# Second expert routing moved into attention, with expert rows and results scattered by indirect DMA

## The reference

```python
x = x + 0.5 * ffn(layernorm(x))      # mixture of experts
x = x + attention(layernorm(x))      # convolution, 8 heads, blocks of 128 tokens
x = x + 0.5 * ffn(layernorm(x))      # the same experts again

def ffn(x):                          # 8 experts, hidden width 176
    h = x.reshape(-1, 256)
    probs = softmax(h @ router_w.T)
    vals, idx = top_k(probs, 2)
    vals = vals / vals.sum(axis=-1, keepdims=True)
    ...
    for each expert e:
        gate, up = split(h @ gup[e].T)
        out += combine[:, e] * ((silu(gate) * up) @ dp[e].T)
```

## Time and profile before

| | us |
|---|---|
| three runs | 907.18, 909.76, 909.19 (median 909.19) |
| the profiled execution, as timed | 907.88 |
| its span in the profile | 905.7 |
| mean granted TensorE clock | 0.905 of 2.4 GHz |

### The profile page before, as it was taken

The page is one execution under the profiler, slowest core; times in us unless marked ns, Lnnn a source line. Parts: engine busy times, 40 slices in busy tenths (PEclk is TensorE's granted clock), DMA queues, the critical chain, the costliest instruction groups (busy, mean ns, idle before and its releaser), DMA issues. The chain is left out here.

```text
span 905.7 us, 20908 instructions
## 1 busy us (share of the span) xinstructions
PE 677.2 (75%) x5582; PEld 613.6 (68%) x5614; DVE 571.1 (63%) x1593; ACT 438.6 (48%) x1624; POOL 398.6 (44%) x449
## 2 busy tenths in 40 slices
PE   3760679999995899999999999852599999950000
PEld 3760569999994678788888888752599999950000
DVE  6668946666665667667676676649666666633333
ACT  1350036666663567677676767640056666630000
POOL 2054645445425544434434321203554444427765
PEclk9999999999996999999999999965599999985555
DMA  9910024444432111111111100000034444424444
GB/s 327 249 60 0 0 79 132 127 130 131 132 100 75 54 42 42 38 48 41 43 38 41 46 20 13 19 24 0 23 115 127 131 127 130 127 84 140 130 135 128
DMA packets 56143, 78.12 MB, mean 86 GB/s; under 512 B 9235, under 2 KB 45973, under 8 KB 56085
## 3 DMA queue, kind: packets, MB, share of 16 engines
q1 hardware_dynamic: 43028, 41.65, 14.1%
q0 software_dynamic: 13056, 35.67, 14.1%
HBM read 45.83 MB, written 31.46 MB: 85 GB/s over the span
## 5 line engine op out<-in xcount | busy, mean ns | idle before, releaser
L495 POOL DMA_INDIRECT shared<-h_rows,stage x144 | 137.7, 956 | 129.2 <-issue 76.0
L528 POOL TENSOR_TENSOR pr<-pr,prec 128x1024 f32<-128x1024 f32 x32 | 60.7, 1897 | 156.0 <-DVE prec L949 156.0
L749 DVE SCALAR_TENSOR_TENSOR x_sb<-yg,wts,x_sb 128x256 f32 (+1 forms) x128 | 62.1, 485 | 71.9 <-DMA yg<-y_rows,cstage 50.1
L1087 PE MATMUL CC<-w_hi,rowsT_hi 128*128 x288 | 106.5, 370 | 0.0
L1087 PE MATMUL CC<-w_lo,rowsT_hi 128*128 x288 | 93.9, 326 | 0.0
L1087 PE MATMUL CC<-w_hi,rowsT_lo 128*128 x288 | 93.8, 326 | 0.0
L648 ACT ACTIVATE pr<-SS,nmax 128x128 f32<-128x128 f32 x256 | 90.6, 405 | 0.1
L861 DVE TENSOR_TENSOR shared<-shared,CC 128x176 f32<-128x176 f32 x144 | 48.6, 337 | 59.4 <-ACT shared L573 43.0
L573 ACT ACTIVATE shared<-CC 128x176 f32<-128x176 f32 x144 | 45.8, 318 | 74.5 <-PE CC L1087 71.5
L540 POOL DMA_INDIRECT yg<-y_rows,cstage x64 | 62.7, 980 | 35.7 <-POOL cstage L535 25.2
L515 POOL DMA_INDIRECT yg<-y_rows,cstage x64 | 62.9, 983 | 23.8 <-issue 16.8
(11 more groups left out here) (211 smaller groups left out, 1983.3 us busy)
## 6 DMA issues: line engine op xcount, KB each, us to landing
y_rows<-shared SPq DMA_DIRECT2D x144, 128.0 KB
x_sb<-in_x_dram SPq DMA_DIRECT2D x4, 1024.0 KB, 8.7
h_rows<-hr SPq DMA_DIRECT2D x32, 128.0 KB, 1.7
out_dram<-x_sb SPq DMA_DIRECT2D x16, 256.0 KB
w_lo<-in_gupT_dram SPq DMA_DIRECT2D x1, 2816.0 KB
shared<-h_rows,stage POOLq DMA_INDIRECT x144
h_rows<-h_ring SPq DMA_DIRECT2D x2, 1024.0 KB, 5.4
h_rows<-pr SPq DMA_DIRECT2D x2, 1024.0 KB, 6.4
```

Of the source, the lines that this page charges most:

```text
L495: pool.indirect_dma_start(out=rows[:, u, :], out_offset=None, in_=h_dram[:, :], in_offset=bass.IndirectOffsetOnAxis(ap=stage[:, k, u:u + 1 ...
L528: pool.tensor_tensor(pr[:, q, :, :], pr[:, q, :, :], prec[:, q, :].unsqueeze(2).to_broadcast([P, NH, P]), ALU.mult).then_inc(t["norm"], 1)
L749: st.did(v.scalar_tensor_tensor(out=x_tile(t), in0=yg[:, q, k, :], scalar=wts[:, k, bass.ds(t, 1)], in1=x_tile(t), op0=ALU.mult, op1=ALU.add))
L1087: i = pe.matmul(CC[:, 512 * (u % 2):512 * (u % 2) + GU], rows_part[:, u % 2, c * P:(c + 1) * P], weights, start=(n == 1), stop=(n == 3 * DC))
```

## The change

**Routing inside attention.** The second routing stage is gone. In the turns that `PICKS` lists, VectorE selects the two experts for four blocks at once (`pick`; for two or one at the end), TensorE counts by small matmuls how many earlier tokens chose the same expert, VectorE fetches these ranks (`read_ranks`) and works out a row number (`place`). Each expert has a region of `REGION` rows in a new DRAM tensor `h_regions`, so no slot has to be known: the row is the expert's region plus the rank. In the turns that `SENDS` lists GpSimd scatters each block's rows there, once for each of its two experts. A row carries two more numbers, so it is 258 wide: twice its token's number, and its first expert. `hr` is a ring of eight in place of two and is no longer stored by SP. After attention `finish_route` works out where each slot tile begins, and SP writes eight tiles of padding behind the experts' rows; eight more are written at the start of attention.

**Expert stage.** SP loads each tile of rows contiguously from its region, at an address from a register. A new operation on VectorE (`y_to`) works out from the two extra numbers to which row each result goes, twice the token's number plus 0 or 1. GpSimd scatters the results there (`send_sums`). Padding rows get a number out of bounds and are left out.

**Last sum.** The results lie in token order, so SP loads them contiguously, two blocks at a time, into the place of the expert weights, which are no longer needed. No ring limits these loads.

**Loops.** Attention is written out turn by turn, and six expert steps stand ahead of the loop in place of two.

The core of the diff:

```diff
...
+        PICKS = {9: (0, 4), 13: (4, 4), 17: (8, 4), 21: (12, 4), 25: (16, 4), 29: (20, 4), 31: (24, 2), 33: (26, 2),
+                 35: (28, 2), 36: (30, 1), 37: (31, 1)}
+        SENDS = {**{b + 10: (b,) for b in range(16)}, 26: (16, 17), 27: (18, 19), 30: (20, 21), 31: (22, 23, 24, 25),
+                 33: (26, 27), 35: (28, 29), 36: (30,), 37: (31,)}
...
+        def turns(turn):
+            for i in range(FIRST_TURN, LAST_TURN):
+                turn(i)
...
+                regs = [sp.alloc_register(f"pad_at{e}") for e in range(E)]
+                sp.load(regs, pad_i[0:1, :])
+                for e in range(E):
+                    at = sp.snap(regs[e], min_val=e * REGION, max_val=e * REGION + TOKENS)
+                    sp.dma_start(h_regions[bass.ds(at, P), :], pad_rows[:, :]).then_inc(T["pads"], 16)
+
...
+                        if s >= RING:
+                            sp.wait_ge(r["rowsT"], s + 1)
+                            sp.wait_ge(r["dest"], s - RING + 1)
+                        sp.dma_start(rows[:, s % RING, :], h_regions[bass.ds(at, P), :]
+                                     ).then_inc(r[f"g{s % RING}"], 16)
+
+            def load_sums():
+                for g in range(TILES // 2):
+                    sp.dma_start(y_pairs(g), y_tokens[:, 2 * g:2 * g + 2, :]).then_inc(y_in[g // 2], 16)
...
             end_phase(sp, 2)
-            store_second()
+            fill_spare()
+            fill_pads()
             end_phase(sp, 3)
+            load_rows(1)
             end_phase(sp, 4)
-            store_y(1)
-            end_phase(sp, 5)
+            load_sums()
...
+                with pool.Fori(0, SLOT_TILES // RING) as j:
+                    for u in range(RING):
+                        pool.wait_ge(r["y_sb"], RING * j + u + 1 + 2)
+                        pool.sem_inc(r["gate_pool"], 1)
+                        pool.wait_ge(r["dest"], RING * j + u + 1)
+                        pool.sem_inc(r["gate_pool"], 1)
+                        pool.indirect_dma_start(
+                            out=y_dram[0:TOPK * TOKENS, :],
+                            out_offset=bass.IndirectOffsetOnAxis(ap=y_dest[:, u:u + 1], axis=0),
+                            in_=y_sb[:, u, :], in_offset=None, bounds_check=TOPK * TOKENS - 1, oob_is_err=False
+                        ).then_inc(r[f"st{u}"], 16)
+                for u in range(RING):
+                    pool.wait_ge(r[f"st{u}"], 16 * (SLOT_TILES // RING))
...
+                    for b in SENDS.get(i, ()):
+                        q = b % GROUP
+                        pool.wait_ge(t["dest"], b + 1)
+                        pool.sem_inc(t["gate"], 1)
+                        for k in range(TOPK):
+                            pool.indirect_dma_start(
+                                out=h_regions[:, :],
+                                out_offset=bass.IndirectOffsetOnAxis(ap=dest[:, q, k:k + 1], axis=0),
+                                in_=hr[:, q, :], in_offset=None).then_inc(t[f"sent{q}"], 16)
...
+                for t in range(TILES):
+                    if t % 4 == 0:
+                        v.wait_ge(y_in[t // 4], 32)
+                    for k in range(TOPK):
+                        st.did(v.scalar_tensor_tensor(out=x_tile(t), in0=y_pairs(t // 2)[:, t % 2, k * D:(k + 1) * D],
+                                                      scalar=wts[:, k, t:t + 1], in1=x_tile(t),
+                                                      op0=ALU.mult, op1=ALU.add))
+                        st.wait()
+                    v.sem_inc(final, 1)
...
+            def finish_route(L):
+                r, t = R[L], T
...
+                step(v.tensor_tensor(passed, etcum[:, :].unsqueeze(1).to_broadcast([P, SLOT_TILES, E]),
+                                     iota_f[:, 0:SLOT_TILES].unsqueeze(2).to_broadcast([P, SLOT_TILES, E]), ALU.is_le))
+                step(v.tensor_reduce(expert_of[:, :], passed[:, :, 0:E - 1], AX.X, ALU.add))
...
+                step(v.scalar_tensor_tensor(out=row_i[:, :], in0=iota_f[0:1, 0:SLOT_TILES], scalar=float(P),
+                                            in1=eidf[:, :], op0=ALU.mult, op1=ALU.add))
...
+                def y_to(u, s, grp):
+                    q = u % RING
+                    v.wait_ge(r[f"g{q}"], 16 * (grp + 1))
+                    after(v, r[f"st{q}"], 16 * grp)
+                    v.scalar_tensor_tensor(out=y_dest[:, q:q + 1], in0=rows[:, q, D + 1:D + 2],
+                                           scalar=expert_of[:, bass.ds(s, 1)], in1=rows[:, q, D:D + 1],
+                                           op0=ALU.not_equal, op1=ALU.add).then_inc(r["dest"], 1)
...
                 def step(u, s, j):
                     if is_tile(s + 1):
                         rows_low((u + 1) % 2, s + 1)
+                        if send:
+                            y_to(u + 1, s + 1, (u + 1) // RING + j)
                     if is_tile(s):
                         hid_s(u % 2, s)
                     if is_tile(s - 1):
...
+                def pick(first, n):
...
+                    v.wait_ge(t["lg"], first + n)
+                    v.sem_inc(passed_dve, 1)
+                    for j in range(at_4, at_4 + n):
+                        ins = v.max(best4[:, j, :], lg4[:, j, :])
+                    step(ins)
+                    step(v.tensor_tensor(oh4[:, of, :, :],
...
+                    v.tensor_tensor(sel4[:, of, :], oh4[:, of, 0, :], oh4[:, of, 1, :], ALU.add
+                                    ).then_inc(t["picked"], n)
+                    v.tensor_scalar(region4[:, of, :], pick4[:, of, :], float(REGION), float(E * REGION),
+                                    ALU.mult, ALU.add)
+
...
+                def read_ranks(first, n):
+                    of = slice(first % 4, first % 4 + n)
+                    v.wait_ge(t["ranked"], first + n)
+                    v.tensor_tensor(rank4[:, of, :, :], oh4[:, of, :, :],
+                                    G[:, D:D + n * E].rearrange("p (i e) -> p i e", e=E).unsqueeze(2)
+                                    .to_broadcast([P, n, TOPK, E]), ALU.mult).then_inc(t["ranks_read"], n)
...
+                def place(first, n):
+                    at_4, q = first % 4, first % GROUP
+                    of = slice(at_4, at_4 + n)
+                    v.wait_ge(t["ranks_read"], first + n)
+                    st.did(v.tensor_reduce(place4[:, of, :], rank4[:, of, :, :], AX.X, ALU.add))
...
+                    v.tensor_tensor(dest[:, q:q + n, :], region4[:, of, :], place4[:, of, :], ALU.add
+                                    ).then_inc(t["dest"], n)
...
                                         negate=True).then_inc(t["max"], 1)
+                    if i in PICKS:
+                        pick(*PICKS[i])
+                    if placed(i, False):
+                        place(*placed(i, False))
...
+                    if i in PICKS:
+                        read_ranks(*PICKS[i])
+                    if placed(i, True):
+                        place(*placed(i, True))
...
+                    if i in PICKS:
+                        first, n = PICKS[i]
+                        at_4 = first % 4
+                        pe.wait_ge(t["picked"], first + n)
+                        after(pe, t["res"], upto(i - 1))
+                        if i > 35:
+                            pe.wait_ge(t["dest"], first)
+                        pe.matmul(G[:, D:D + n * E], before_bf[:, :], sel4[:, at_4:at_4 + n, :], start=True, stop=False,
+                                  skip_group_check=True)
+                        for j in range(n - 1):
...
+                        pe.matmul(G[:, D:D + n * E], ones_bf[:, :],
+                                  so_far[:, :].unsqueeze(1).to_broadcast([P, n, E]), start=False, stop=True,
+                                  skip_group_check=True).then_inc(t["ranked"], n)
+
+                turns(turn)
+                pe.wait_ge(t["dest"], TILES)
+                pe.matmul(G[:, D:D + E], ones_bf[:, :], so_far[:, :], start=True, stop=True).then_inc(t["counted"], 1)
...
```

272 lines of the change are left out of this document (165 added, 107 removed).

## The result

The changed kernel takes 967.9 us (median of four runs, 963.9 to 971.5) against 909.0 us for the kernel before beside it. The ratio is 1.065, with a 95% interval of 1.060 to 1.070. The forecast was 929 us and the range 888 to 960: the sign was right, the size was not, and the time lies outside the range. The profiled execution has a span of 967.6 us, timed at 969.3.

The account below looks back on a forecast made before the run. VectorE was taken to bound the second routing, TensorE the second expert stage. The sum 905.7 - 3 + 70 - 46 = 926.7, with 2.2 around the span, gave 929 us; range 888 to 960.

Parts of the forecast that it names:

- Part 1: Up to the second expert stage's first transposes: gain 3 us; a gain of 18 or loss of 12 not excluded.
- rival (c): Routing in attention not hidden: scatters delay every turn's normalisation, or the tail is longer; 15 us more, 944 us; chance 0.12.
- Part 2: Second expert stage: tiles take 3.1 us in place of 2.07, for 68 tiles; 70 us added.
- The loop: Second expert stage: VectorE's index operation for tile k waits for tile k-4's scatter; 6.2 us for two tiles.
- Part 3: Last sum, from the last expert eviction to the end: 53.7 us in place of 99.8, a gain of 46.
- (a): Second expert stage: scatter lands quickly enough, breaking even at 1.91 us; kernel faster, 883 us at the lower bound; chance 0.21.
- (b): Second expert stage: the loop binds and TensorE's clock falls; 97 us added, 956 us; chance 0.13.
- (d): Second expert stage: index operation never late, its semaphore old by then; 2.07 us a tile, 859 us; chance 0.02.

Follow-up runs that it names:

- two edits: Changed kernel with one y_dest column for each tile in place of a ring of four, 890.7 us; changed kernel with y_to moved last in its step, 920.4 us.
- 72 columns: Changed kernel with one column of y_dest for each of the 72 tiles in place of a ring of four: 890.7 us, 0.980 of the kernel before.

## Why the prediction was wrong

**Part 1, the turns.** The step that failed is the sentence that GpSimd's two scatters a turn fit a turn of 9.25 us. By occupancy they do: GpSimd idles 3.4 us in each such turn. What they do to the turn does not show in any sum of durations: they make a row of four indirect transfers, and TensorE's signals fall into it. It costs 30.2 us (with and without scatters), where rival (c) had set aside 15 for turns and tail together and a chance of 0.12. A second error lay the other way: a pick of four blocks was put at 2.2 us, 13 in all, and costs 1.0, 5.7 in all. The selection takes 2.5 us and not 3.1, and the sentence that there is no slack behind it was wrong: in the turn with a pick, VectorE's wait for TensorE ahead of `qk` shrinks from 0.79 to 0.21 us, and that ahead of `mhaT` by 0.16.

**Part 1, the tail.** Right in its parts: block 31's normalisation later by 7.5 us, measured 8.2; from there to the last `dest` 26.2 us, measured 24.0. From the last `dest` to the first transposes 11.1 was said, and 14.8 came: the last pad landed 3.4 us after its issue, within the bounds of 1.7 and 5.5, and the eight stores, each at a place from a register, took 6 us to issue. GpSimd's drain at the change of stage, which is not in the sum, runs from 667.66 to 676.54 and ends only 0.7 us before that pad has landed, so quicker pads alone would have gained no more than that. The 12 us by which a loss was not excluded were meant for such things; the turns alone went past it.

**Part 1, the start.** 6.4 us ahead of attention were not in the sum. Of these, 3.2 are inside the stage. At least 1.3 of them, and probably most, are the spare tiles' stores, which the kernel issues at the start of that stage and which I costed at nothing without naming their cover. The other 3.1, ahead of the first expert stage, have no cause shown.

**Part 2.** The mechanism is right and shown by two edits. The loop was put at 6.2 us for two tiles and is 6.48 in the round below; from the fifth tile on the transposes are 3.22 us apart on average. From the chain of the changed kernel:

```profile
747.31 2.69 DMA y_rows<-shared,y_dest
750.90 0.26 DVE hidB L964
751.40 0.38 PE SS L1272
752.38 0.39 ACT shared L647
753.79 2.59 DMA y_rows<-shared,y_dest
```

Landing 2.69 us where the gather's 2.54 stood in for it, VectorE to the end of the eviction 2.77 (2.84 said), from there to the scatter 1.02 (0.83 said). An error of 0.14 us a tile is 9.5 us over 68 tiles: a loop that turns 34 times asks for better than 5%. Of the 72 scatters 65 land 2.1 to 2.7 us after their start, the slowest after 4.8, with a median of 2.56. The Trainium skill (DMA: Bandwidth & Descriptors, Anatomy of one DMA — SWDGE (gpsimd) path) gives a fixed 2.0 us and bytes over 436 GB/s, 2.3 us for 128 KB as an estimate, and the trace agrees in size.

**Part 3.** 53.7 said, 54.0 measured, but by two errors that cancel. The way from the last eviction to the first load was put at 3.7 us, with 0.3 for the change of stage, and took 9.3, of which GpSimd's drain is 5.95; the additions were put at 1.3 us a block, 41.6 in all, and run at 1.15, 36.7 us from 928.04 to 964.8. That the part came out right is luck.

**Rivals.** (a) fell with the landing time: it needed 1.91 us, and no scatter of the stage landed in less than 2.07. (b) did not come: TensorE at 0.78 busy kept a granted clock of 0.97. (d) is what the kernel becomes with 72 columns: the 859 us given for it would have been 887 with the other parts as they are (967.9 less the 80.7 by which the stage had grown), and 890.7 were measured. The chance of faster was put at 0.25, and nearly all of it was on the scatter's landing.

## What to carry to other kernels

A wait that is put on an engine in front of work for other tiles closes a loop; its price is the round trip over the number of tiles that the order lets it gain, and a deeper ring for a tiny index buffer removes it altogether, here 77 us for 272 bytes a partition. To move work "into slack", free time on the issuing engine is not enough: look at what falls into its busy stretch on the others, and place bursts where nobody waits. A change of stage has a price of its own, here 5.9 us for GpSimd's drain ahead of the last sum. Work that is moved to the end of a stage goes behind the last item that others wait for, not ahead of it.
